# Two self attentions on one Trainium2 core: four batches per score product, ScalarE drains the diagonal, softmax skewed by a tile

## What is computed

```python
q, k, v = (xn @ Wq), (xn @ Wk), (xn @ Wv)          # each to (B, 16 heads, 32, 32)
scores = einsum('bhqd,bhkd->bhqk', q, k) / sqrt(32)
attn = softmax(scores, axis=-1)
o = einsum('bhqk,bhkd->bhqd', attn, v)             # then @ Wo and the residual
```

## Time and profile before

| | |
|---|---|
| median of 3 runs | 2062.92 us (2062.58 to 2063.96) |
| the profiled execution | 2063.49 us |
| its span in the trace | 2061.7 us |
| PE busy | 1865.9 us, 91% |
| DVE busy | 916.8 us, 44% |
| ACT busy | 615.8 us, 30% |
| POOL busy | 152.3 us, 7% |

### The profile page before, as it was taken

The page is one execution under the profiler, slowest core; times in us unless marked ns, Lnnn a source line. Parts: engine busy times, 40 slices in busy tenths (PEclk is TensorE's granted clock), DMA queues, the critical chain, the costliest instruction groups (busy, mean ns, idle before and its releaser), DMA issues.

```text
span 2061.7 us, 37699 instructions
## 1 busy us (share of the span) xinstructions
PE 1865.9 (91%) x16852; PEld 1530.2 (74%) x16852; DVE 916.8 (44%) x1353; ACT 615.8 (30%) x1144; POOL 152.3 (7%) x241
## 2 busy tenths in 40 slices
PE   5889789998668999899999999998964899999999
PEld 4635678877557887788888888886754688888887
DVE  4415654362454656254444444446134643433323
ACT  2211352243324112233333333332511233322321
POOL 1301500010000001100000000021100100000000
PEclk9999799999769999999999999998975899999999
DMA  5394001111101111101111111111110011111101
GB/s 183 141 371 160 21 21 67 41 46 41 43 3 37 46 41 41 63 22 33 32 41 32 32 32 32 33 32 47 46 39 4 1 62 41 42 62 41 62 21 41
DMA packets 43170, 113.35 MB, mean 55 GB/s; under 512 B 4320, under 2 KB 21088, under 8 KB 36480
## 3 DMA queue, kind: packets, MB, share of 16 engines
q1 hardware_dynamic: 43008, 110.92, 15.6%
HBM read 108.74 MB, written 2.10 MB: 54 GB/s over the span
## 4 chain that ended last, share of the span: by engine, by line
PE 80%; DVE 8%; issue 7%; ACT 3%; POOL 1%; DMA 0%; SPq 0%; POOLq 0%; DVEq 0%; ACTq 0%
PE PS L610 22%; PE PS L611 22%; PE PS L612 22%; PE PS L955 3%; PE PS L838 2%; DVE pool_area L1775 2%; PE PS L969 2%; PE PS L717 1%; PE PS L738 1%; PE PS L971 1%; PE PS L852 1%; ACT SCP L1073 1%; DVE bns L1381 1%; PE PS L947 1%; PE PS L625 1%
## 5 line engine op out<-in xcount | busy, mean ns | idle before, releaser
L610 PE MATMUL PS<-T1h,Wh 128*128 128x512 f32 x768 | 305.0, 397 | 17.0 <-DVE T1l L1457 11.9
L611 PE MATMUL PS<-T1l,Wh 128*128 128x512 f32 x768 | 303.6, 395 | 0.0
L612 PE MATMUL PS<-T1h,Wl 128*128 128x512 f32 x768 | 303.3, 395 | 0.0
L610 PE MATMUL PS<-Wh,B1h 128*128 128x512 f32 x608 | 238.8, 393 | 0.0
L612 PE MATMUL PS<-Wh,B1l 128*128 128x512 f32 x608 | 236.7, 389 | 0.0
L611 PE MATMUL PS<-Wl,B1h 128*128 128x512 f32 x608 | 236.7, 389 | 0.0
L610 PEld LDWEIGHTS PS<-T1h,Wh 128*128 128x128 f32 x768 | 147.3, 192 | 49.6 <-DVE T1l L1457 13.0
L1043 ACT CAST Wh<-W 128x2048 fp32r<-128x2048 f32 x51 | 97.3, 1908 | 287.5 <-PE PS L612 276.5
L1443 DVE TENSOR_TENSOR Wl<-W,Wh 128x2048 fp32r<-128x2048 f32 x51 | 116.8, 2291 | 146.4 <-ACT Wh L1043 146.4
L612 PEld LDWEIGHTS PS<-T1h,Wl 128*128 128x128 f32 x768 | 147.0, 191 | 31.2
L611 PEld LDWEIGHTS PS<-T1l,Wh 128*128 128x128 f32 x768 | 147.1, 192 | 30.7
(11 more groups left out here) (245 smaller groups left out, 3133.2 us busy)
## 6 DMA issues: line engine op xcount, KB each, us to landing
W<-units_dram SPq DMA_DIRECT2D x51, 1024.0 KB, 4.9
pool_area<-ctx_t_dram SPq DMA_DIRECT2D x32, 512.0 KB, 4.3
T1f<-ctx_dram SPq DMA_DIRECT2D x25, 512.0 KB, 6.5
H<-ctx_t_dram SPq DMA_DIRECT2D x15, 516.0 KB, 7.9
T1f<-ctx_t_dram SPq DMA_DIRECT2D x12, 516.0 KB, 7.0
pool_area<-ctx_dram SPq DMA_DIRECT2D x7, 512.0 KB, 6.0
pool_area<-ctx_t_dram SPq DMA_DIRECT2D x5, 516.0 KB, 8.9
X<-x_dram SPq DMA_DIRECT2D x8, 256.0 KB, 5.2
```

The source lines that it names most:

```text
L610: nc.tensor.matmul(out_, a[0], b[0], start=first, stop=False)
L611: nc.tensor.matmul(out_, a[0], b[1], start=False, stop=False)
L612: return nc.tensor.matmul(out_, a[1], b[0], start=False, stop=last)
```

## The change

The scores of one head are taken for all four batches of a tile in one product of 32x128 by 32x128, with a result of 128x128: 16 products for a tile, 32 in the second self attention. Of each result the four diagonal squares are used, so ACT drains them in four instructions on 32 partitions each, in both self attentions. The causal mask is then added by DVE in `SCP`. The scores now always take banks 0 to 3, the values banks 4 to 7. The values of a tile are multiplied two tiles behind the scores, and DVE's work is in two parts: `centre` of tile t, then `normalise` of tile t-1, then `low_values` of tile t-2. The transposed probabilities go to `XN`, and `SCP` is a ring of four.

```diff
-    for t in range(T + 1):
+    for t in range(T + 2):
         if t < T:
-            J.add(("s3", t), "act", banks=4)
-        if t >= 1:
-            J.add(("o3", t - 1), "dve", banks=4, split=True)
+            J.add(("s3", t), "act", banks=4, at=0)
+        if t >= 2:
+            J.add(("o3", t - 2), "dve", banks=4, split=True, at=4)
...
-            J.add(("s5", t), "dve", banks=4)
-        if t >= 1:
-            J.add(("o5", t - 1), "dve", banks=4, split=True)
+            J.add(("s5", t), "act", banks=4, at=0)
+        if t >= 2:
+            J.add(("o5", t - 2), "dve", banks=4, split=True, at=4)
...
                 for hb in range(C):
-                    for hl in range(HG):
-                        hs = slice(hl * DK, (hl + 1) * DK)
-                        for j in range(PB):
-                            js = slice(j * SEQ, (j + 1) * SEQ)
-                            ts = slice(t * P + j * SEQ, t * P + (j + 1) * SEQ)
-                            for i, (a, k) in enumerate(pairs):
-                                mm = nc.tensor.matmul(bk[js, hl, hb * SEQ:(hb + 1) * SEQ], a[hs, hb, ts], k[hs, hb, ts],
-                                                      start=(i == 0), stop=(i == len(pairs) - 1))
+                    for i, (a, k) in enumerate(pairs):
+                        for hl in range(HG):
+                            hs = slice(hl * DK, (hl + 1) * DK)
+                            mm = nc.tensor.matmul(bk[:, hl, hb * P:(hb + 1) * P], a[hs, hb, tok(t)], k[hs, hb, tok(t)],
+                                                  start=(i == 0), stop=(i == len(pairs) - 1))
...
-                if t >= 1:
-                    pe.wait_ge(prob_ready, prob["s3", t - 1])
-                    self_values("o3", t - 1, A2t, SCP[:, 2 + (t - 1) % 2, :])
+                if t >= 2:
+                    pe.wait_ge(prob_ready, prob["s3", t - 2])
+                    self_values("o3", t - 2, A2t, xn(t))
...
+            def own_scores(name, t):
+
+                if t >= NTMP:
+                    act.wait_ge(prob_ready, prob[name, t - NTMP])
+                act.wait_ge(ready, J.ready[name, t])
+                bk = banks((name, t), 4)
+                for j in range(PB):
+                    js = slice(j * SEQ, (j + 1) * SEQ)
+                    ins = nc.scalar.activation(SCP[js, t % NTMP, :].rearrange("p (l h k) -> p l h k", l=HG, h=C),
+                                               bk[js, :, :].rearrange("p l (h j k) -> p l h j k", h=C, j=PB)[:, :, :, j, :],
+                                               ACT.Copy, scale=float(DK) ** -0.5)
+                    if j == PB - 1:
+                        ins.then_inc(act_drained, 1)
+                    else:
+                        step(ins)
+
+            def attend(name, values):
+
+                own_scores(name, 0)
+                for t in range(T + 2):
+                    if t + 1 < T:
+                        own_scores(name, t + 1)
+                    if t < T:
+                        act.wait_ge(bias_ready, soft[name, t])
+                        nc.scalar.activation(SCP[:, t % NTMP, :], SCP[:, t % NTMP, :], ACT.Exp).then_inc(exp_ready, 1)
                     if t >= 2:
-                        act.wait_ge(prob_ready, prob["s3", t - 2])
...
+                        high_values(values, t - 2)
...
+            def attend(name, values, causal):
+
+                for t in range(T + 2):
+                    if t < T:
+                        centre(name, t, causal)
+                    if 1 <= t <= T:
+                        normalise(name, values, t - 1)
+                    if t >= 2:
+                        low_values(values, t - 2)
```

More of the change, by code:

```diff
@@ L991, in _ @@
             wait(("qj", G - 1, C - 1))
-            for t in range(T + 1):
+            for t in range(T + 2):
                 if t < T:
                     self_scores("s5", t, [(A0, A1), (QJ, A3)])
-                if t >= 1:
-                    pe.wait_ge(prob_ready, prob["s5", t - 1])
-                    self_values("o5", t - 1, A2t, SCP[:, 2 + (t - 1) % 2, :])
+                if t >= 2:
+                    pe.wait_ge(prob_ready, prob["s5", t - 2])
+                    self_values("o5", t - 2, A2t, xn(t))
             wo5 = wait_unit("4.o")
@@ L1173, in _ @@
             next_after("2.v")
-            for t in range(T + 1):
-                if t < T:
-                    if t >= 2:
-                        act.wait_ge(prob_ready, prob["s3", t - 2])
[L1178 to L1185, removed]
+            def own_scores(name, t):
[14 more added lines that the diff above has]
+                own_scores(name, 0)
+                for t in range(T + 2):
+                    if t + 1 < T:
[3 more added lines that the diff above has]
+                        nc.scalar.activation(SCP[:, t % NTMP, :], SCP[:, t % NTMP, :], ACT.Exp).then_inc(exp_ready, 1)
+                    if t >= 2:
+                        high_values(values, t - 2)
+            attend("s3", "o3")
             def high_relu(b, g):
@@ L1284, in _ @@
             next_after("4.v")
[L1285 to L1290, removed]
+            attend("s5", "o5")
             for t in range(T - TAIL):
@@ L1642, in _, with centre, normalise @@
             next_after("2.v")
-            def softmax(name, t, SC, PTs):
+            def centre(name, t, causal):
+                SC = SCP[:, t % NTMP, :]
                 s3 = SC.rearrange("p (h k) -> p h k", k=SEQ)
-                link(nc.vector.reduce_max(tiny[:, 1, 0:HEADS], s3, AX_X))
-                nc.vector.tensor_tensor(s3, s3, bc(tiny[:, 1, 0:HEADS].unsqueeze(2), P, HEADS, SEQ), ALU.subtract).then_inc(bias_ready, 1)
+                dve.wait_ge(act_drained, J.drain[name, t][1])
+                if causal:
+                    link(nc.vector.tensor_tensor(SC.rearrange("p (l n) -> p l n", l=HG), SC.rearrange("p (l n) -> p l n", l=HG),
+                                                 bc(con_("causal").unsqueeze(1), P, HG, P), ALU.add))
+                top = tiny[:, 1, 48 * (t % 2):48 * (t % 2) + HEADS]
+                link(nc.vector.reduce_max(top, s3, AX_X))
+                nc.vector.tensor_tensor(s3, s3, bc(top.unsqueeze(2), P, HEADS, SEQ), ALU.subtract).then_inc(bias_ready, 1)
+            def normalise(name, values, t):
+                SC = SCP[:, t % NTMP, :]
+                s3 = SC.rearrange("p (h k) -> p h k", k=SEQ)
                 dve.wait_ge(exp_ready, exps[name, t])
@@ L1653, in softmax @@
                 if t >= 2:
-                    dve.wait_ge(ready, J.ready[{"s3": "o3", "s5": "o5"}[name], t - 2])
-                nc.vector.transpose(PTs, SC).then_inc(prob_ready, 1)
+                    dve.wait_ge(ready, J.ready[values, t - 2])
+                nc.vector.transpose(XN[:, t % 2, :], SC).then_inc(prob_ready, 1)
+            def attend(name, values, causal):
+                for t in range(T + 2):
+                    if t < T:
+                        centre(name, t, causal)
+                    if 1 <= t <= T:
+                        normalise(name, values, t - 1)
+                    if t >= 2:
+                        low_values(values, t - 2)
             exps = {}
@@ L1667, in _ @@
             exps["sig"] = len(exps) + 2
[L1669 to L1674, removed]
+            attend("s3", "o3", False)
             def out3_drain(t):
@@ L1806, in _ @@
             next_after("4.v")
[L1807 to L1817, removed]
+            attend("s5", "o5", True)
             def out5_drain(t):
```

## The result

The changed kernel takes 2074.74 us (median of 4 runs, 2073.67 to 2079.29) against 2062.75 in the same runs for the kernel before: a ratio of 1.0061, 95% interval 1.0045 to 1.0076. It is slower by 12 us; 2044.4 was forecast, in a range of 2031 to 2062. The profiled execution took 2074.71 us with a span of 2072.5, so the span grew by 10.8 from that of the earlier trace rows.

The account below looks back on a forecast made before the run. Instruction fetch was taken to bound PE in both self attentions; 0 in the first and -19 us in the second, with half a us for packet ends, gave -18.5: 2063.5 to 2045.0, median 2044.4, range 2031 to 2062.

Parts of the forecast that it names:

- The fetch fits: PE idles 4.2 us in each turn, in which a packet arrives: Both self attentions: instruction packets of 256 arrive while PE waits, so fetch adds almost nothing to a turn.
- the holes: PE's waits for instructions ("issue") at packet ends, some 2 us each; expected nearly gone from both self attentions.
- two packets are held after a wait: PE's instruction queue: some two packets of 256 instructions held in advance after a long wait, then run without a hole.
- The 234 records: First self attention before: 234 score records, 468 instructions, start in 2.2 us, then nothing for 1.87 us, taken as fetch.
- My slower rival: Both self attentions: holes stay, 1.25 or 1.5 of 2 us on top of each turn; +25 us, chance 0.04.
- The ring's turn of 7.25 and 8.95 us: Time per tile in the two self attentions for values, scores, drains, exponential, high and low part waiting on one another.
- 127.6 forecast: Forecast for both self attentions together: 58.0 us in the first and 69.6 us in the second.
- The two unknown values: Score products in both self attentions: four row groups run side by side, and the clock stays at its lower level.
- The first stage unchanged, the whole gain in the second: First self attention 58.0 us, as much as before; second 69.6 us, 19.0 less than 88.63.
- The bound before: Both self attentions before: PE bound by instruction fetch, 256 per 3.57 us; 57 and 86 us against 57.95 and 88.63.
- The rival with the full clock: Clock back at full in the busier stage: turns 6.4 and 7.25 us, -29 us, chance 0.14.
- the one with three groups: Score products overlap only as three row groups: turns 7.8 and 10.1 us, -8.5 us, chance 0.19.

Follow-up runs that it names:

- shift48: Changed kernel with twelve repeated small score products (48 records) in tile 0 of the first self attention; 2060.63 us, ratio 0.9983.
- The shifts: Changed kernel with 4, 8, 12 or 32 repeated small score products in tile 0 of the first self attention; 2066.87, 2069.82, 2060.63, 2061.11 us.
- merged_again: merged_only run once more, for its profile; 2032.59 us, ratio to the kernel before 0.9842.
- merged_only: Changed kernel's merged scores and four drains, but in the old order: values one tile behind, softmax in one piece; 2030.18 us, ratio 0.984.
- high_first: Changed kernel with one edit: ACT takes the high part of tile t-2 ahead of the four drains of tile t+1; 2037.01 us, ratio 0.9875.
- shift16: Changed kernel with four repeated small score products (16 records) in tile 0 of the first self attention; 2066.87 us, ratio 1.0012.
- shift32: Changed kernel with eight repeated small score products (32 records) in tile 0 of the first self attention; 2069.82 us, ratio 1.0026.
- half_values: Changed kernel with the values products of heads hl = 2 and 3 left out, half the values not computed; 2043.66 us (one run).

## Why the prediction was wrong

- **"The fetch fits: PE idles 4.2 us in each turn, in which a packet arrives"** is the step that failed. PE idles 4.7 us, and the holes are 22.6 us instead of about 2 (1 in each stage). As idle time that is +20 us; in shift48, 17.1 us less of holes made both stages 13.7 us shorter. A stop for the low part soon behind a boundary doesn't fetch ahead: during the idle time before 563.20, from 558.0 to 563.1, the trace has no packet of the instruction queue; one comes between 563.1 and 566, and the hole ends at 566.56:

```profile
q8 instruction: 1, 0.02, 2.1%
```

  From the earlier trace rows I had read that two packets are held after a wait. The 234 records had a long stretch of large products ahead of them. The stop before 548.22 also comes 22 matmuls behind a boundary, but it is for the probabilities, and from 545.0 to 548.1, during the stop, the trace has

```profile
q8 instruction: 1, 0.02, 1.9%
```

  I carried this over to a stop for the low part, which behaves otherwise. The shifts show that where PE stops counts, not only how long, and merged_again that it matters for what it stops. My slower rival, with chance 0.04, had a hole at every boundary; half of it was right.
- **The ring's turn of 7.25 and 8.95 us** was right in its parts, and too small in all but one. Measured from 573.65 to 581.89: values 1.46 (1.3), scores 2.09 (1.7), to ACT 0.13 (0.2), drains 2.45 (2.2), exponential 0.66 (0.54), high part 0.61 (0.59), low part and handover 0.84 (0.75), sum 8.24. I had taken durations from start to start for work whose full length lies on the path. In the second stage a turn without a hole takes 9.9. Over both stages that is about the rest: 157.1 less 127.6 forecast less 20.6 of holes, +9.
- **The two unknown values** were right: four score records do run side by side (in the second stage of shift48 eight start from 1573.85 to 1574.28, one every 0.053 us = 0.214/4; a tile's 32 take 2.09 us, where one by one they would take 32 x 0.214 = 6.8), and the clock stayed at its lower level in the first stage (0.54) and for most of the second (0.60).
- **"The first stage unchanged, the whole gain in the second"**: the first lost 16.2 us and the second gained 5.7. In the first a ring of 8.24 us and its holes stand against a turn before of 7.1, in the second against 11.07.
- **The bound before** was named rightly. merged_only and merged_again show that with fewer instructions the same order runs 31 to 34 us faster.
- **Slips in the working**: the parts of the ring add to 7.28, not 7.25. The rival with the full clock counts its gain over four turns (58.0-54.6 = 4 x 0.85), the one with three groups its loss over nearly six (3.4 over 0.6). Neither decides the outcome.
- The Trainium skill, "Runtime: NRT & Kernel Launch", Instruction fetch mechanics, says that the sequencer fetches the next block while it runs the present one. The traces agree in that one block is asked for ahead, no more: the packets come one for each block passed. "Mostly hidden" holds for the large products of L610 to L612, which show a single "issue" of 0.8 us from 600 to 1500 us; these stages show 2.0 to 2.4 us for most crossings that aren't hidden.

I also had the ring in the prediction, with its 4 us of idle PE in each turn, and did not ask which link could be moved. high_first moves one and wins 37.7 us.

## What to carry to other kernels

When a change makes an engine's list wait in a new order, write down the ring, then look for the link that stands there only by the order of one list: here the high part, whose input was ready 5 us before its turn. Where small products are bound by the fetch of instructions, count 256 at a time and mark where PE stops and for what: a stop soon behind a boundary can hold back the next block, so idle time in a turn doesn't by itself pay for a fetch. A change that moves many small instructions should be timed at two or three shifts of them, since 4 to 32 products that do nothing moved this kernel by 5 to 14 us.

## What the runs showed of the hardware

- Holes of 2.0 to 2.4 us at block boundaries after stops of 1.6 to 4.7 us, and of 0.85 and 1.51 in a busy stretch (changed kernel). With stops for the low part 15 to 26 matmuls behind a boundary, the next one was a hole (changed kernel); in the first stage 33 matmuls were enough (shift16), in the second 34 and 35 were not (shift32), and 8 more were (shift48). With stops for the probabilities 22 matmuls (before, 548.22) and 26 behind one (merged_again, 591.19), the packet came during the stop. Counted on from the changed kernel's boundaries, half_values stops some 24 behind one in its first stage and 18 in its second, for the low part, and has no hole. What sets the distance stays open.
- Four drains on 32 partitions take 2.43 us, 0.61 each, one on 128 partitions 0.60: a drain on a quarter of the partitions takes as long as one on all.
